# Two-layer attention kernel: bf16 planes stored once and repeated by their loads, and a new order of the work in slots 0 to 6

## Chip, cores and metric

The kernel runs on one core of one Trainium2 chip. The metric is the device time of one launch in microseconds. Below, PE is TensorE, DVE is VectorE, ACT is ScalarE, POOL is GpSimd, and SP is SyncE, which here only issues DMAs.

## The reference

Input x is (8, 128, 64, 64) in fp32. Each of the 8 images goes through two layers.

```
# layer 0 (on the Haar bands of x, 32x32 pixels, N0 = 1024)
ll_out  = sparse attention on ll: 8 heads of 16, q and k l2-normalized,
          keep the top half of each row of q.k, softmax, times v, 1x1 conv, group norm
high    = h + alpha * GN(1x1(silu(GN(depthwise3x3(h)))))      # h: the other three bands
out     = x + 0.1 * inverse_haar(ll + ll_out, high)
out     = out + 0.1 * GN(1x1(gelu(GN(1x1(out)))))
# layer 1 (on 64x64 pixels, N1 = 4096, queries and keys of 16 channels)
attn    = softmax(q.k / 4);  result = gamma * (Wo (v.attn) + bo) + out
```

## The kernel before

**Images overlap.** While image b is in layer 0 (one head per slot), image b-1 is in layer 1 (one chunk of 512 queries per slot). `slots(b, l0, l1)` issues 8 such slots, and `between(f, n, fin, opn)` lies between two images: it finishes layer 0 of image f and opens image n. Image 0 runs alone in layer 0 (`alone`), and the last image alone in layer 1 (`chunks`). The first chunk's maxima are issued by `first`, the last slot by `closing`; the others by `search(h)` and the statements in the loop over h.

**The order is written out by hand.** Each engine has its own list of calls (`search` on PE and DVE, the loop body on ACT), and every engine works strictly in its list's order. They are tied by semaphores.

**A slot, layer 0, head h.** `score` (PE, L446, banks 0 and 1) makes a row block of q.k, `evict` (ACT, L1175) copies it out and sums it, `centre` (DVE) makes thresholds, `count` (ACT, L1183, 24 per head) counts entries above them, and `apart`, `flip`, `eight` (DVE, L1743, L1751, L1760), `match`, `middle`, `threshold` find the exact median. `turn` (PE), `turned` (ACT, L1217) and three DMAs put it as three extra rows under the queries. `half_t` (PE, L514) then makes the transposed scores in halves, `half_e` (ACT, L1235) takes exp, `half_m` (DVE, L1857) masks, and `weigh` (PE, L524) multiplies with v. `score(h + 1, 0)` waits for the last `half_m` of head h - 1.

**A slot, layer 1, chunk j.** `maxima` (PE L548, DVE L1928, 32 per chunk) finds each query's largest score, `parts` and `maxrow` (DVE, PE L555, ACT L1251) split it and move it into QP1, `l1_score` (PE L566), `l1_exp` (ACT L1243) and `l1_weigh` (PE L582) do the attention, and `l1_norm`, `l1_turn` (PE L594), `l1_out` (DVE L1960) end the chunk.

**Planes.** To multiply fp32 values in bf16, q and k are split into three bf16 planes (p0, p1, p2). `TERMS` lists six pairs (plane of q, plane of k), so the contraction has 6 x 16 = 96 rows. Before the change `store_planes` (L286) writes each plane to DRAM once for every term and side that uses it, twelve stores per image, and `load_head` (L279) reads a head's 96 rows with two loads. Layer 1 has one copy of its planes in DRAM (L406) and twelve loads (L410) of 16 rows each into QP1 and KP1. All of these are issued by SP in `between`, after a wait for the last plane (p12) in layer 1. The first `maxima` of a chunk row waits for all of the loads (`qp1`) and for the evicted values (`v1c`); layer 0's first `score` waits for `hq0`.

The one place where the shape of a DMA is set is this (L286, L410):

```python
sp.dma_start(scr0[w, :, j, :, :], PT[:, t, w * N0:w * N0 + N0]).then_inc(s["scrw"], 16)
sp.dma_start(dst[16 * j:16 * j + 16].rearrange("p (j n) -> p j n", j=4),
             scr1[t].rearrange("(j s) n -> s j n", s=32)[16 * w:16 * w + 16]).then_inc(s["qp1"], 16)
```

Of the kernel before, what the change touches and what calls it, by code (L numbers as in the profile page):

```python
# [7 lines left out]
N1 = H * W  # L8
HH = H // 2
N0 = HH * HH  # L10
# [7 lines left out]
TERMS = [(0, 0), (0, 1), (1, 0), (1, 1), (0, 2), (2, 0)]  # L18
# [80 lines left out]
def dwt_attention_kernel(nc, x, qkvT, projT, dw, pwT, w1T, w2T, qk1T, wv, woT, vec, cst, cstT, out,  # L99
# [4 lines left out]
    with ctx:  # L104
# [148 lines left out]
        def kp(h):  # L253
# [4 lines left out]
          scrw1 qp1 v1p v1c m mr mp mt mpt mq st1 e1 pv1 on nt xr0 xr1 y1 out0 out1 dset dimg dpr pimg g1 g2 g3 g4  # L258
# [6 lines left out]
        def _(sp):  # L265
# [10 lines left out]
            def load_head(h):  # L276
                done = s["hq%d" % (h % 3)]
                for w in range(2):
                    sp.dma_start(QK0[0:KS, h % 3, w, :], scr0[w, h].rearrange("j d n -> (j d) n")).then_inc(done, 16)  # L279

            def store_planes(n, t, made):
                sp.wait_ge(s[made], (n + 1) * 2)
                for j, pair in enumerate(TERMS):
                    for w in range(2):
                        if pair[w] == t:
                            sp.dma_start(scr0[w, :, j, :, :], PT[:, t, w * N0:w * N0 + N0]).then_inc(s["scrw"], 16)  # L286
# [2454 lines left out]
```

## Time and profile before

| what | us |
|---|---|
| median of 3 runs | 5668.78 |
| lowest and highest run | 5662.02, 5674.28 |
| span of the profiled execution | 5667.7 |
| span around which the prediction's sum is made, against the median | 1.1 less |

For the profiled execution the page gives its span and no time of its own beside it.

| engine | busy us | share of the span |
|---|---|---|
| PE | 4766.2 | 84% |
| DVE | 4618.9 | 81% |
| ACT | 4256.4 | 75% |
| POOL | 250.6 | 4% |

The 16 DMA engines are busy for 11% of the span. Busy means that an instruction of the engine is executing; PE's ends are modelled. A released wait is named after the instruction whose end released it.

### The profile page before, as it was taken

What the parts mean: (1) busy time and instruction counts of PE and PEld (TensorE: products, weight loads), DVE (VectorE), ACT (ScalarE), POOL (GpSimd) and SP (SyncE); (2) the same over time, 40 slices, a digit from 0 to 9 for tenths busy, and PEclk for the clock granted to TensorE, in tenths of its full rate; (3) what the DMA queues carried; (4) which work ended last, traced back from release to release, by engine and by line L of the source; (5) the groups of instructions that cost most, each with busy time, mean ns of one, the idle gap of its engine ahead of it and who ended that gap; (6) DMA issues with size and microseconds to landing.
All of it is one profiled execution on the core that took longest, in us unless ns stands there. A gap on an engine that the chain in (4) does not pass through costs nothing.

```text
span 5667.7 us, 92692 instructions
## 1 busy us (share of the span) xinstructions
PE 4766.2 (84%) x30180; PEld 3123.3 (55%) x30180; DVE 4618.9 (81%) x9087; ACT 4256.4 (75%) x6779; POOL 250.6 (4%) x125
## 2 busy tenths in 40 slices
PE   4444899988999889988999889998899889997799
PEld 2001366654666456663666546664466636664588
DVE  4887799987999789986999879997799879996553
ACT  3883699948998499966999489884899669994333
POOL 2001000010000200010000100002000100000000
PEclk7555799998999989998999989999899989998899
DMA  1001200012001110012000120011100120001100
GB/s 68 7 11 50 74 15 16 15 56 76 16 20 43 59 43 18 16 61 74 15 15 13 58 76 16 20 43 50 51 16 18 59 75 15 15 13 43 36 12 16
DMA packets 104805, 199.97 MB, mean 35 GB/s; under 512 B 36632, under 2 KB 41656, under 8 KB 100184
## 3 DMA queue, kind: packets, MB, share of 16 engines
q1 hardware_dynamic: 104280, 193.56, 11.1%
q8 instruction: 257, 4.21, 0.3%
q14 instruction: 268, 2.20, 0.1%
HBM read 110.61 MB, written 82.05 MB: 34 GB/s over the span
## 4 chain that ended last, share of the span: by engine, by line
PE 41%; DVE 23%; ACT 15%; issue 14%; SPq 3%; DMA 3%; DVEq 0%; ACTq 0%; POOL 0%; POOLq 0%
PE PS L582 16%; ACT work L1183 7%; PE PS L548 5%; DVE M L1760 4%; DVE MX L1928 4%; PE PS L566 4%; ACT work L1243 3%; DVE work L1751 3%; PE PS L514 3%; PE PS L524 3%; DVE work L1743 2%; PE PS L1057 2%; ACT arena L1175 2%; DVE arena L1857 2%; DMA work<-TPT 1%
## 5 line engine op out<-in xcount | busy, mean ns | idle before, releaser
L582 PEld LDWEIGHTS PS<-V,work 128*128 128x128 f32 x16384 | 2106.7, 193 | 155.8 <-issue 7.0
L582 PE MATMUL PS<-V,work 128*128 128x129 f32 x16384 | 2125.2, 277 | 2.5 <-ACT work L1243 1.2
L1183 ACT ACTIVATE work<-arena,T 128x1024 bf16<-128x1024 f32 x1504 | 1725.8, 1150 | 22.7 <-DVE T L1671 18.8
L1928 DVE TENSOR_REDUCE MX<-PS 128x1 f32<-128x512 f32 x2048 | 1399.3, 687 | 249.6 <-PE PS L548 233.9
L1243 ACT ACTIVATE work<-PS 128x1024 f32<-128x1024 f32 x1024 | 1046.8, 1024 | 334.0 <-PE PS L566 332.3
L548 PE MATMUL PS<-KP,QP 96*128 96x512 bf16 x2048 | 845.5, 414 | 137.3 <-DVE MX L1928 95.3
L566 PE MATMUL PS<-QP,KP 99*128 99x512 bf16 x2048 | 624.6, 387 | 77.5 <-ACT work L1243 54.2
L1175 ACT ACTIVATE arena<-PS 128x1024 f32<-128x1024 f32 x512 | 523.2, 1022 | 216.7 <-PE PS L446 209.5
L1857 DVE SCALAR_TENSOR_TENSOR arena<-PS,work 128x512 f32<-128x512 f32 x896 | 606.2, 684 | 67.3 <-ACT work L1235 65.3
L1760 DVE MAX8 M<-work 128x8 f32<-128x512 f32 x1024 | 648.4, 682 | 1.0
L1235 ACT ACTIVATE work<-PS 128x512 f32<-128x512 f32 x896 | 530.8, 601 | 119.9 <-PE PS L514 116.1
L548 PEld LDWEIGHTS PS<-KP,QP 96*128 96x128 bf16 x2048 | 200.5, 98 | 543.8 <-DVE MX L1928 419.1
L446 PE MATMUL PS<-work 96*128 96x512 bf16 x1024 | 350.5, 428 | 175.2 <-ACT arena L1175 167.2
L514 PE MATMUL PS<-work 99*128 99x512 bf16 x896 | 337.3, 388 | 93.7 <-DVE arena L1857 54.2
L1743 DVE TENSOR_SCALAR work<-arena,T 128x1024 f32<-128x1024 f32 x512 | 378.4, 745 | 2.3
L1751 DVE TENSOR_SCALAR work<-work,FL 128x1024 uint32<-128x1024 uint32 x512 | 375.9, 747 | 1.0
L524 PE MATMUL PS<-arena,VT 128*17 128x256 f32 x4096 | 321.4, 411 | 10.0 <-DVE arena L1849 5.8
L566 PEld LDWEIGHTS PS<-QP,KP 99*128 99x128 bf16 x2048 | 185.0, 99 | 222.6 <-ACT work L1243 126.5
L1183 ACT ACTIVATION_READ_ACCUMULATOR work<-arena,T 128x1 f32 x1504 | 302.9, 201 | 0.0
L446 PEld LDWEIGHTS PS<-work 96*128 96x128 bf16 x1024 | 80.4, 102 | 329.9 <-ACT arena L1175 272.2
L514 PEld LDWEIGHTS PS<-work 99*128 99x128 bf16 x896 | 83.2, 98 | 222.1 <-DVE arena L1857 127.0
L2614 POOL TENSOR_TENSOR work<-work 128x1024 f32<-128x1024 f32 x8 | 22.5, 2814 | 3509.9 <-DMA work<-in_x 3509.9
(193 smaller groups left out, 4160.8 us busy)
## 6 DMA issues: line engine op xcount, KB each, us to landing
scr<-work SPq DMA_DIRECT2D x96, 256.0 KB
work<-scr SPq DMA_DIRECT2D x128, 192.0 KB, 2.8
work<-in_x SPq DMA_DIRECT2D x16, 1024.0 KB, 7.7
arena<-in_x SPq DMA_DIRECT2D x8, 2048.0 KB, 9.9
scrX<-arena SPq DMA_DIRECT2D x8, 2048.0 KB, 14.2
XR<-scrX SPq DMA_DIRECT2D x64, 256.0 KB, 2.8
out<-YO SPq DMA_DIRECT2D x64, 256.0 KB, 2.0
scrL<-work SPq DMA_DIRECT2D x24, 512.0 KB, 2.6
```

Source lines behind the costliest of these rows:

```text
L514: mm(PS[:, c, :], kp(h)[0:KA, 128 * mt:128 * mt + 128], qp(h)[0:KA, 512 * c:512 * c + 512], start=True, stop=True).then_inc(s["st" if c el ...
L548: mm(PS[:, maxbank(c, k, l0), :], QP1[0:KS, c * 512 + 128 * i:c * 512 + 128 * i + 128], KP1[0:KS, 512 * w:512 * w + 512], start=True, stop ...
L566: last = mm(PS[:, pairbanks(k, l0) + t, :], KP1[0:KA, 128 * mt:128 * mt + 128], QP1[0:KA, j * 512:j * 512 + 512], start=True, stop=True)
L582: last = mm(PS[:, 5 + i // 2, 136 * (i % 2):136 * (i % 2) + 129], P1[:, (16 * j + k) % 3, t, 128 * i:128 * i + 128], V1[:, mt, :], start=( ...
L1175: A(scores(h, i), bank2(0), ACT.Copy, scale=0.25, accum_out=SUM[:, h % 2, i:i + 1]).then_inc(s["eva"], 1)
L1183: A(junk[:, m % 2, :], scores(h, i), ACT.Sign, scale=-1.0, bias=T[:, h % 2, i:i + 1], accum_out=CA[:, h % 2, i:i + 1]).then_inc(s["ca"], 1)
L1235: A(JA[:, mt % 2, 512 * c:512 * c + 512], PS[:, c, :], ACT.Exp, scale=0.25).then_inc(s["e" if c else "eh"], 1)
L1243: A(P1[:, (16 * j + k) % 3, :, :].rearrange("p t n -> p (t n)"), PS[:, u:u + 2, :].rearrange("p a n -> p (a n)"), ACT.Exp, scale=0.25).the ...
L1751: cp.did(V.tensor_scalar(JDu[:, c, :], JDu[:, c, :], FL[:, h % 2, i:i + 1].bitcast(u32), None, ALU.bitwise_xor))
L1760: cp.did(V.max(M8[:, i, a, :], JD[:, c, 512 * a:512 * a + 512]))
L1857: V.scalar_tensor_tensor(scores(h, mt)[:, 512 * c:512 * c + 512], PS[:, c, :], 0.0, JA[:, mt % 2, 512 * c:512 * c + 512], ALU.is_ge, ALU.m ...
L1928: V.reduce_max(MX[:, c % 2, i, w:w + 1], PS[:, maxbank(c, k, l0), :], AX.X).then_inc(s["mr"], 1)
```

## The change

The planes of layer 0 are kept once in DRAM (scr0 by plane, partition, side) and stored by one DMA per plane. A head's rows are put together by seven loads, some of which read a plane two or three times, or read two planes at once. `TERMS` is reordered so that rows that share a plane lie together. Layer 1's planes are stored in rows of 8 KB, each plane as soon as it exists, and loaded by seven DMAs in place of twelve. Waits on the counts of these semaphores are adapted. Head 0 of the next image is loaded before its third plane is ready; rows of that plane go from SBUF to SBUF.

The lists of slots 0 to 6 on PE, DVE and ACT have the same calls in another order. `first`, `closing`, `alone`, `chunks` and `between` on these engines are as before.

```diff
-TERMS = [(0, 0), (0, 1), (1, 0), (1, 1), (0, 2), (2, 0)]
+TERMS = [(0, 0), (0, 1), (0, 2), (1, 0), (1, 1), (2, 0)]
-        scr0 = nc.dram_tensor("scr0", [2, NH, len(TERMS), HD, N0], bf16, kind="Internal").ap()
-        scr1 = nc.dram_tensor("scr1", [3, 128, N0], bf16, kind="Internal").ap()
+        scr0 = nc.dram_tensor("scr0", [3, 128, 2, N0], bf16, kind="Internal").ap()
+        scr1 = nc.dram_tensor("scr1", [3, 32, N1], bf16, kind="Internal").ap()
...
-            def load_head(h):
+            def load_head(h, parts=(0, 1, 2)):
                 done = s["hq%d" % (h % 3)]
-                for w in range(2):
-                    sp.dma_start(QK0[0:KS, h % 3, w, :], scr0[w, h].rearrange("j d n -> (j d) n")).then_inc(done, 16)
-
-            def store_planes(n, t, made):
+                d = slice(HD * h, HD * h + HD)
+                q, k = QK0[0:KS, h % 3, 0, :], QK0[0:KS, h % 3, 1, :]
+                if 0 in parts:
+                    sp.dma_start(q[0:48], scr0[0, d, 0, :].unsqueeze(0).to_broadcast([3, HD, N0])).then_inc(done, 16)
+                    sp.dma_start(k[80:96], scr0[0, d, 1, :]).then_inc(done, 16)
+                if 1 in parts:
+                    sp.dma_start(k[0:32], scr0[0:2, d, 1, :]).then_inc(done, 16)
+                    sp.dma_start(k[48:80], scr0[0:2, d, 1, :]).then_inc(done, 16)
+                    sp.dma_start(q[48:80], scr0[1, d, 0, :].unsqueeze(0).to_broadcast([2, HD, N0])).then_inc(done, 16)
+                if 2 in parts:
+                    sp.dma_start(q[80:96], scr0[2, d, 0, :]).then_inc(done, 16)
+                    sp.dma_start(k[32:48], scr0[2, d, 1, :]).then_inc(done, 16)
+
+            def store_plane(n, t, made):
                 sp.wait_ge(s[made], (n + 1) * 2)
-                for j, pair in enumerate(TERMS):
-                    for w in range(2):
-                        if pair[w] == t:
-                            sp.dma_start(scr0[w, :, j, :, :], PT[:, t, w * N0:w * N0 + N0]).then_inc(s["scrw"], 16)
+                sp.dma_start(scr0[t].rearrange("p w n -> p (w n)"), PT[:, t, :]).then_inc(s["scrw"], 16)
+
+            def head0_late():
+                for w, row in ((0, 80), (1, 32)):
+                    sp.dma_start(QK0[row:row + HD, 0, w, :], PT[0:HD, 2, w * N0:w * N0 + N0]).then_inc(s["hq0"], 16)
...
                 if opn:
-                    store_planes(n, 0, "p0")
-                    store_planes(n, 1, "p1")
-                    store_planes(n, 2, "p2")
+                    store_plane(n, 0, "p0")
+                    store_plane(n, 1, "p1")
                     sp.wait_ge(s["vt"], (n + 1) * 2)
                     sp.sem_inc(s["free"], 1)
-                    sp.wait_ge(s["scrw"], (n + 1) * 192)
-                    for h in range(3):
+                    sp.wait_ge(s["scrw"], n * 48 + 32)
+                    load_head(0, (0, 1))
+                    store_plane(n, 2, "p2")
+                    head0_late()
+                    sp.wait_ge(s["scrw"], (n + 1) * 48)
+                    for h in range(1, 3):
                         load_head(h)
                 if fin:
-                    sp.wait_ge(s["p12"], f + 1)
-                    for a in range(3):
-                        sp.dma_start(scr1[a], PT1[:, a, :]).then_inc(s["scrw1"], 16)
-                    sp.wait_ge(s["scrw1"], (f + 1) * 48)
-                    for j, (tq, tk) in enumerate(TERMS):
-                        for w, (t, dst) in enumerate(((tq, QP1), (tk, KP1))):
-                            sp.dma_start(dst[16 * j:16 * j + 16].rearrange("p (j n) -> p j n", j=4),
-                                         scr1[t].rearrange("(j s) n -> s j n", s=32)[16 * w:16 * w + 16]).then_inc(s["qp1"], 16)
+                    for a, made in enumerate(("p10", "p11", "p12")):
+                        sp.wait_ge(s[made], f + 1)
+                        sp.dma_start(scr1[a].rearrange("s (j n) -> j s n", j=4), PT1[:, a, :]).then_inc(s["scrw1" if a < 2 else "scry1"], 16)
+                    sp.wait_ge(s["scrw1"], (f + 1) * 32)
+                    planes = scr1.rearrange("t (w d) n -> t w d n", w=2)
+                    sp.dma_start(KP1[0:32], planes[0:2, 1]).then_inc(s["qp1"], 16)
+                    sp.dma_start(KP1[48:80], planes[0:2, 1]).then_inc(s["qp1"], 16)
+                    sp.dma_start(KP1[80:96], planes[0, 1]).then_inc(s["qp1"], 16)
+                    sp.dma_start(QP1[0:48], planes[0, 0].unsqueeze(0).to_broadcast([3, HD, N1])).then_inc(s["qp1"], 16)
+                    sp.dma_start(QP1[48:80], planes[1, 0].unsqueeze(0).to_broadcast([2, HD, N1])).then_inc(s["qp1"], 16)
+                    sp.wait_ge(s["scry1"], (f + 1) * 16)
+                    sp.dma_start(KP1[32:48], planes[2, 1]).then_inc(s["qp1"], 16)
+                    sp.dma_start(QP1[80:96], planes[2, 0]).then_inc(s["qp1"], 16)
...
@@ PE, the loop over h
+                    l1_weigh(h - 1, 15, (0,))
+                    last_weigh(h, 7)
+                    l1_weigh(h - 1, 15, (1,))
                     maxrow(h)
...
```

**SP in `between`, layer 1's planes.** Here QP and KP are QP1 and KP1, arena holds PT1 and X1, scr is scr1. Before, three stores and the first of twelve loads:

```order
L406 DMA scr<-arena 128x1024 x3
L407 REGISTER_ALU
L410 DMA QP<-scr 16x4x1024
L410 DMA KP<-scr 16x4x1024
...
L413 ISA
```

After:

```order
L420 DMA scr<-arena 4x32x1024 x3
L421 REGISTER_ALU
L423 DMA KP<-scr 32x1x4096
L424 DMA KP<-scr 32x1x4096
L425 DMA KP<-scr 16x4096
L426 DMA QP<-scr 48x1x4096
L427 DMA QP<-scr 32x1x4096
L428 REGISTER_ALU
L429 DMA KP<-scr 16x4096
L430 DMA QP<-scr 16x4096
```

Four loads now fill 32 or 48 rows each, three fill 16 rows, and the store's outermost dimension in DRAM is 4.

**ACT at the end of a slot.** L1235 (L1249 after) is `half_e`, L1183 (L1196) is `count`, L1251 (L1265) is `maxrow`, L1175 (L1188) is `evict` of the next head, L1243 (L1257) is `l1_exp`. Before:

```order
L1235 ACTIVATE work<-PS 128x512
L1182 REGISTER_ALU
L1183 ACTIVATE work,CA<-arena,T 128x1024
L1235 ACTIVATE work<-PS 128x512
L1250 REGISTER_ALU
L1251 ACTIVATE MPT<-PS 12x128
L1203 ISA
L1175 ACTIVATE arena,SUM<-PS 128x1024
L1240 REGISTER_ALU
L1243 ACTIVATE work<-PS 128x1024
```

After:

```order
L1196 ACTIVATE work,CA<-arena,T 128x1024
L1249 ACTIVATE work<-PS 128x512
L1195 REGISTER_ALU
L1196 ACTIVATE work,CA<-arena,T 128x1024
...
L1264 REGISTER_ALU
L1265 ACTIVATE MPT<-PS 12x128
L1217 ISA
L1188 ACTIVATE arena,SUM<-PS 128x1024
L1217 REGISTER_ALU
L1188 ACTIVATE arena,SUM<-PS 128x1024
```

Three counts now stand between the last `half_e` of the slot and `maxrow` (one is shown, two are left out), and two evictions follow each other.

**PE at the end of a slot.** L555 (L574 after) is `maxrow`, L582 (L601) is `l1_weigh`, L524 (L543) is `weigh`, L446 (L465) is `score` of the next head, L594 (L613) is `l1_turn`. Before:

```order
L514 MATMUL PS<-work 128x512
L555 MATMUL PS<-identb,MP 12x128
L573 REGISTER_ALU
L582 MATMUL PS<-V1,work 128x129 x8
L524 MATMUL PS<-arena,VT 17x256 x12
L473 ISA
L446 MATMUL PS<-work 128x512 x2
L594 MATMUL PS<-cons,ON 128x128 x4
```

After:

```order
L601 MATMUL PS<-V1,work 128x129 x8
L574 MATMUL PS<-identb,MP 12x128
L492 ISA
L465 MATMUL PS<-work 128x512 x2
L543 MATMUL PS<-arena,VT 17x256 x12
L613 MATMUL PS<-cons,ON 128x128 x4
L482 REGISTER_ALU
L465 MATMUL PS<-work 128x512 x2
```

The next head's first score stands ahead of three `weigh` calls now, and its second one behind `l1_turn`.

## Rows read from the trace of the kernel before

**Rows 1.** The page's first line.
```profile
span 5667.7 us, 92692 instructions
```
**Rows 2.** Busy time by stretch of one slot: us, PE, PEld, DVE, ACT, POOL busy; PE clock, DMA share, GB/s.
```profile
1498.10:1561.90 63.80, 58.72 (x430) 41.77 (x428) 59.09 (x122) 59.21 (x100) 0.00 (x0) 1.00 0.06 19
...
1498.10:1528.40 30.30, 26.76 (x185) 18.73 (x184) 28.82 (x62) 28.70 (x48) 0.00 (x0) 1.00 0.06 22
1528.40:1534.00 5.60, 4.75 (x35) 3.73 (x33) 3.75 (x8) 5.34 (x10) 0.00 (x0) 1.00 0.01 2
1534.00:1558.80 24.80, 24.10 (x179) 17.43 (x177) 23.92 (x46) 24.15 (x42) 0.00 (x0) 1.00 0.06 15
1558.80:1561.90 3.10, 3.10 (x37) 1.89 (x36) 2.60 (x8) 1.01 (x2) 0.00 (x0) 1.00 0.19 47
```
**Rows 3.** Waits in two slots, 1498.1 to 1625.6: us in total, times, longest.
```profile
ACT arena L1175 <- PE PS L446: 10.2, 7, 2.7
...
DVE MX L1928 <- PE PS L548: 4.0, 8, 0.9
```
**Rows 4.** ACT in that slot: start, us, instruction, idle before it and releaser.
```profile
1529.13 0.25 ACT L1217 ACTIVATE TPT<-PS 24x128 bf16<-24x128 f32 x1
...
1530.42 1.13 ACT L1183 ACTIVATE work<-arena,T 128x1024 bf16<-128x1024 f32 x1
...
1533.04 0.60 ACT L1235 ACTIVATE work<-PS 128x512 f32<-128x512 f32 x1 [0.26 <-PE PS L514]
...
1560.89 1.02 ACT L1175 ACTIVATE arena<-PS 128x1024 f32<-128x1024 f32 x1 [2.70 <-PE PS L446]
```
**Rows 5.** DVE in that slot.
```profile
1528.21 0.17 DVE L1843 TENSOR_TENSOR TP<-TR,TP 128x8 bf16<-128x8 f32 x1
...
1534.00 0.68 DVE L1857 SCALAR_TENSOR_TENSOR arena<-PS,work 128x512 f32<-128x512 f32 x1
...
1557.43 0.74 DVE L1743 TENSOR_SCALAR work<-arena,T 128x1024 f32<-128x1024 f32 x1
1558.11 0.69 DVE L1857 SCALAR_TENSOR_TENSOR arena<-PS,work 128x512 f32<-128x512 f32 x1
```
**Rows 6.** PE at the end of that slot.
```profile
1556.84 2.05 PE L582 MATMUL PS<-V,work 128*128 128x129 f32 x16
1558.82 1.49 PE L524 MATMUL PS<-arena,VT 128*17 128x256 f32 x24
1560.24 0.61 PE L446 MATMUL PS<-work 96*128 96x512 bf16 x2
```
**Rows 7.** SP's DMA issues between images 1 and 2: start, us, issues.
```profile
1290.92 13.92 SPq L286 DMA_DIRECT2D scr<-work  x12
...
1317.86 1.32 SPq L406 DMA_DIRECT2D scr<-arena  x3
```
**Rows 8.** Stretches in which one kind of DMA runs; last two columns: DMA share, GB/s.
```profile
11.00:13.00 2.00, 0.00 (x0) 0.00 (x0) 0.00 (x0) 0.00 (x0) 2.00 (x1) 1.00 1.00 422
...
1305.00:1309.40 4.40, 2.52 (x6) 1.06 (x6) 4.40 (x5) 3.77 (x5) 0.00 (x0) 1.00 0.50 195
...
1208.00:1210.00 2.00, 2.00 (x18) 1.72 (x17) 1.00 (x2) 1.49 (x3) 2.00 (x2) 1.00 0.42 143
```
**Rows 9.** The three planes' last instructions, layer 0 (p1, p2), layer 1 (p12).
```profile
1291.28 2.00 ACT L1518 ACTIVATE work<-work 128x1024 bf16<-128x1024 f32 x2
...
1300.77 1.21 DVE L2409 TENSOR_TENSOR work<-work 128x1024 bf16<-128x1024 f32 x1
...
1316.61 1.23 DVE L2371 TENSOR_TENSOR arena<-arena 128x1024 bf16<-128x1024 f32 x1 [0.26 <-ACT arena L1478]
```
**Rows 10.** PE's first maxima after the loads, images 1/2 and the last.
```profile
1338.21 0.59 PE L548 MATMUL PS<-KP,QP 96*128 96x512 bf16 x2 [0.47 <-ACT V L1484]
1339.37 20.71 PE L548 MATMUL PS<-KP,QP 96*128 96x512 bf16 x30 [0.57 <-DVE MX L1928]
...
5288.58 1.01 PE L548 MATMUL PS<-KP,QP 96*128 96x512 bf16 x2 [13.08 <-DMA KP<-scr]
```

More of the change, by code:

```diff
@@ L435, in _ @@
             for i in range(3):
-                sp.wait_ge(s["hq%d" % i], images * len(range(i, NH, 3)) * 32)
+                sp.wait_ge(s["hq%d" % i], images * len(range(i, NH, 3)) * 112)
             sp.wait_ge(s["dls"], images * 48)
@@ L472, in score @@
                     if i == 0:
[L473 removed]
+                        pe.wait_ge(s["hq%d" % (h % 3)], (b * len(range(h % 3, NH, 3)) + h // 3 + 1) * 112)
                     products(h, i)
@@ L694, in search @@
                     l1_score(h - 1, 10)
                     half_t(h - 1, 1, 1)
+                    maxima(h, 20)
+                    l1_weigh(h - 1, 9, (1,))
+                    half_t(h - 1, 2, 0)
+                    maxima(h, 21)
                     weigh(h - 1, 0)
-                    maxima(h, 21)
-                    l1_weigh(h - 1, 9, (0,))
-                    half_t(h - 1, 2, 0)
+                    weigh(h - 1, 1)
+                    half_t(h - 1, 2, 1)
                     maxima(h, 22)
-                    l1_weigh(h - 1, 9, (1,))
@@ L702, in search @@
-                    half_t(h - 1, 2, 1)
-                    maxima(h, 23)
-                    weigh(h - 1, 1)
                     l1_score(h - 1, 11)
                     half_t(h - 1, 3, 0)
-                    maxima(h, 24)
+                    maxima(h, 23)
                     l1_weigh(h - 1, 10, (0,))
                     half_t(h - 1, 3, 1)
+                    maxima(h, 24)
+                    l1_weigh(h - 1, 10, (1,))
                     maxima(h, 25)
-                    l1_weigh(h - 1, 10, (1,))
@@ L914, in score0 @@
                         pe.wait_ge(s["kon"], n + 1)
-                        pe.wait_ge(s["hq0"], (n * len(range(0, NH, 3)) + 1) * 32)
+                        pe.wait_ge(s["hq0"], (n * len(range(0, NH, 3)) + 1) * 112)
                     products(0, i)
@@ L1377, in slots @@
                     count(h, 1, 5)
+                    l1_exp(h - 1, 9)
                     half_e(h - 1, 0, 0)
+                    half_e(h - 1, 0, 1)
                     count(h, 1, 6)
-                    half_e(h - 1, 0, 1)
-                    count(h, 1, 7)
                     half_e(h - 1, 1, 0)
                     half_e(h - 1, 1, 1)
-                    count(h, 2, 0)
+                    count(h, 1, 7)
                     half_e(h - 1, 2, 0)
@@ L1387, in slots @@
                     half_e(h - 1, 2, 1)
+                    count(h, 2, 0)
+                    l1_exp(h - 1, 11)
+                    half_e(h - 1, 3, 0)
+                    half_e(h - 1, 3, 1)
                     count(h, 2, 1)
-                    half_e(h - 1, 3, 0)
-                    l1_exp(h - 1, 11)
-                    half_e(h - 1, 3, 1)
                     count(h, 2, 2)
+                    count(h, 2, 3)
                     half_e(h - 1, 4, 0)
@@ L1395, in slots @@
                     half_e(h - 1, 4, 1)
-                    count(h, 2, 3)
                     half_e(h - 1, 5, 0)
@@ L2043, in search @@
                     apart(h, 4)
+                    maxima(h + 1, 1)
+                    centre(h + 1, 0)
+                    apart(h, 5)
                     maxima(h + 1, 2)
-                    apart(h, 5)
+                    flip(h, 5)
                     maxima(h + 1, 3)
-                    centre(h + 1, 0)
-                    flip(h, 5)
+                    eight(h, 5)
                     maxima(h + 1, 4)
-                    eight(h, 5)
+                    flip(h, 4)
                     maxima(h + 1, 5)
-                    flip(h, 4)
+                    eight(h, 4)
@@ L2053, in search @@
+                    maxima(h + 1, 6)
                     apart(h, 7)
-                    maxima(h + 1, 6)
-                    eight(h, 4)
                     maxima(h + 1, 7)
                     apart(h, 6)
-                    flip(h, 7)
                     maxima(h + 1, 8)
                     flip(h, 6)
+                    maxima(h + 1, 9)
+                    flip(h, 7)
                     centre(h + 1, 1)
-                    maxima(h + 1, 9)
-                    eight(h, 6)
+                    update(h + 1, 0, 0)
@@ L2064, in search @@
                     maxima(h + 1, 10)
                     eight(h, 7)
-                    update(h + 1, 0, 0)
                     maxima(h + 1, 11)
+                    eight(h, 6)
+                    maxima(h + 1, 12)
                     match(h)
-                    maxima(h + 1, 12)
+                    maxima(h + 1, 13)
                     middle(h)
-                    maxima(h + 1, 13)
                     threshold(h)
                     maxima(h + 1, 14)
+                    update(h + 1, 0, 1)
```

193 lines of the change are left out of this document (87 added, 106 removed).

## Prediction

> **What bounds the kernel now.** I read the page's first line [rows 1], then the timeline, then busy time by stretch. An image takes a passage between two images and eight slots; seven images are worked on in pairs, so 56 slots carry most of the span. In a slot of 63.8 us three engines are busy for almost the same time: PE 58.7, DVE 59.1, ACT 59.2 us [rows 2]. No engine is the bound alone; the slot is longer than any of them by 4.6 to 5.1 us because they wait for each other in turn. The waits say where [rows 3]: ACT waits for the next head's score, up to 2.7 us at a time, and DVE for PE's maxima, 4.0 us in two slots. I cut the slot into three parts. From the last mask of a head to the median (threshold) of the next, 3.1 + 30.3 us, DVE is busiest. From the threshold's end to the first mask, 5.6 us, a chain runs over PE, ACT and DMAs [rows 4, 5]. In the 24.8 us of the masks all three engines are at 23.9 us or more [rows 2]. Then ACT stands idle for 2.70 us [rows 4]: PE first weighs (2.05 and 1.49 us) and only then makes the score for which ACT waits [rows 6].
>
> In the passage between images the first maxima of layer 1 are the gate: behind them DVE reduces 30 blocks in a row, in 20.71 us, and the next slot can't start earlier [rows 10]. They waited for an eviction of values by ACT, not for planes, in the passage shown; in the last image they waited 13.08 us for the load of the planes [rows 10].
>
> **Change, part 1: the slots.** What ACT does stays the same in amount. The masks' part loses three of ACT's counts, 3 x 1.13 = 3.4 us [rows 4], which now fill the idle time behind the last mask; one `apart` of DVE, 0.68 us from start to the next start [rows 5]; and one of PE's weigh halves. DVE then bounds it: 23.9 - 0.7 = 23.2 us of work, and I add 0.2 for one late handoff: 24.8 becomes 23.4, **-1.4 us**. The part up to the threshold gets that `apart`: 33.4 becomes 34.1, **+0.7**. ACT had 28.7 + 1.0 = 29.7 us of work there [rows 2] and gets 3.4 more while one `l1_exp` of 0.9 us leaves it, so 32.2 us: it fits under 34.1, with 1.9 us left for waits. Part of that is spent, since two evictions now follow each other and the second score stands behind `l1_turn`; following the order I find 1.4 us of idle time there. In the chain over the TPT rows ACT has that `l1_exp` ahead of the first `half_e`: 0.25 + 3.4 + 0.9 = 4.5 us against the 3.91 from 1529.13 to 1533.04, less what ACT waited in it (0.26) and what it can start earlier, since it will already stand ready: **+0.1**. Sum -0.6 us a slot. It applies to the six full distances between two slots of each image, 7 x 6 = 42: **-25 us**. The first boundary of an image gains nothing, as `eight(h, 0)` now stands ahead of `parts` there, and `closing` is as before. Bounds of the term: the best is all of DVE's waits for maxima gone, 2.0 us a slot, -84 us; the worst is that ACT's waits grow past the 1.9 us, say by 0.8 us a slot, +34 us.
>
> **Change, part 2: layer 1's planes.** I go through what the most loaded DMA engine must carry. The twelve old stores to scr0 have an outermost dimension of 8 in DRAM, are queued together (12 issues in 13.92 us) [rows 7], and while they drain the 16 engines have a share of 0.50 at 195 GB/s [rows 8]: 8 of 16 engines, 24.4 GB/s each, and the same 8 for all, since otherwise twelve waiting stores would have filled the rest. The load that repeats scrD for seven heads shows 0.42 [rows 8], close to 7 of 16. So the outermost count of the pattern sets how many engines share a DMA. A load that takes two planes (or one plane twice) then has 2 engines, three copies have 3, layer 1's stores have 4. At a share of 1.00 with 8 KB rows the engines move 422 GB/s [rows 8], 26.4 each, so 0.31 us per 8 KB row; at 24.4 GB/s a 2 KB row takes 0.084 us.
>
> The Trainium skill states the same as a rule, against this change (DMA: Bandwidth & Descriptors, "Why a DMA increments its semaphore by 16 and not by 1"): a DMA issued by SP uses the largest number of engines up to 16 that divides the slowest dimension of both sides, and takes the lowest-numbered ones. By that rule the loads pile up on engines 0 and 1; without it, spread over all engines, part 2 would cost nothing. The 0.50 of the trace agrees with it.
>
> The most loaded engine's queue, image 1 to 2: p1 ends at 1293.3 [rows 9], so head 0 is loaded from about 1296 to 1303; p2 ends at 1302.0 [rows 9], its store has landed by about 1305. Then heads 1 and 2 are loaded: per head four loads give it 16 rows each and three give it one, 67 rows x 0.084 = 5.6 us, so it is busy from 1306 to 1317.3. The three stores of layer 1 (p12 ends at 1317.8) [rows 9] give it 32 rows each, 96 x 0.084 = 8.1 us: 1325.4. The seven loads give it 4 x 16 + 3 = 67 rows of 8 KB, 67 x 0.31 = 20.8 us: 1346.2, and landed by 1346.5. PE could have started at 1338.2 [rows 10]: **8.3 us late**. Nothing hides this, since the 30 maxima, the row of maxima and the first score stand in line behind it. ACT's counts don't absorb it: their thresholds come from DVE updates that stand between these maxima. In the last image the same queue, without head loads, ends 8 to 9 us after the old 5288.6. Eight passages: 8 x 8.3 = **+67 us**. Bounds: the loads can't start before the second plane's store has landed, about 1320, which gives 1341, 3 us late (+24); at 21 GB/s per engine the queue ends near 1351, 13 us late (+104). If the engine count is not what I read, the term is 0.
>
> **Small parts.** Layer 0's stores fall from twelve to three, and head 0 is loaded earlier; PE's wait for it in the passage is covered, because ACT evicts layer 1's first planes before it needs that score: 0. A head's seven loads in a slot are issued behind the maxima rows and have 30 us until anything behind them is needed: 0. PE's clock, 1.00 in the slot [rows 2], will fall to its lower level (1.2 GHz) while PE waits for the loads; maxima at 0.69 us each are paced by DVE, so it costs nothing there.
>
> **Sum.** -25 + 67 = +42 us on the profiled execution's 5667.7; it lies 1.1 us under the median of the runs, 5668.8, which gives **5711 us**. About 0.2% (11 us) is what a measurement of this kernel can tell from no change.
>
> **The rivals.**
> - *Planes in time.* The loads run on different engines, or on all 16. For it: a store drawn up with 128 rows on both sides runs on all 16 engines, and nothing in the trace shows a pattern with an outermost count of 2. Against it: the 0.50 and 0.42 [rows 8]. Only the slots' gain is left: 5668.8 - 25 = 5644. It decides from 1338.2 on: if the loads land before that, this is the case. Chance 0.20. This is the other side of my forecast.
> - *The slots give much more.* All DVE waits go, 42 x 2.0 = 84 us, against 67: 5652. The three engines are balanced at 59 us, which speaks for room down to 61.4 us; against it speaks that DVE's maxima pass through one PSUM bank, a round trip each. Break-even is 67/42 = 1.6 us a slot. Chance 0.10.
> - *The slots give nothing or lose.* The second eviction waits for `l1_turn`, which waits for `l1_norm`, and DVE now has one `eight` ahead of it. ACT's idle time of 2.70 us moves there. At no gain 5668.8 + 67 = 5736; at 0.8 us a slot lost, 5769. It decides once ACT waits more than 1.9 us up to the threshold. Chance 0.17.
> - *Forecast*, both parts as worked out: 0.53.
>
> **The numbers.** The forecast's own range is 5668 to 5736, from the bounds of 3 to 13 us with the slots near -0.6. The range 5636 to 5745 adds most of the first two rivals and the milder half of the third; it leaves out some 0.15. Faster by over 0.2%: nearly all of "planes in time" and half of "much more", 0.22. Within 0.2%: 0.10, from the low end of the forecast and the rest of these. Slower: 0.68.
>
> **What the next profile would show.** Right: the first maxima of each passage wait for a DMA into KP1 or QP1, 8 us, at a DMA share near 2/16 over some 20 us; the last image's wait is over 20 us instead of 13.08. A slot takes 63.2 us; ACT has no idle time ahead of the first eviction and about 1.4 us ahead of the second. Wrong: maxima released by ACT's eviction of V as before, or a slot at 63.8 us or above, or at 62 us and below.

## The result and the profile after the change

The changed kernel takes 5750.4 us (median of 4 runs, 5739.3 to 5753.1) against 5665.4 us of the kernel before (4 runs, 5652.9 to 5674.3): a ratio of 1.0151, 95% interval 1.0131 to 1.0172, so **1.5% slower**. Forecast were 5711 us and a range up to 5745: the sign was right, the loss was twice as large.

The page's first line and its groups for the maxima, for the eviction and for one DMA, with the maxima's group of the kernel before behind them, then the time of each slot part (columns as in [rows 2]). The last number of a group is the engine's idle time ahead of it, in us:

```profile
span 5737.5 us, 92907 instructions
...
L567 PE MATMUL PS<-KP,QP 96*128 96x512 bf16 x2048 | 845.7, 414 | 258.0 <-DVE MX L1942 117.6
...
L1188 ACT ACTIVATE arena<-PS 128x1024 f32<-128x1024 f32 x512 | 524.3, 1024 | 116.7 <-PE PS L465 106.7
...
scrX<-arena SPq DMA_DIRECT2D x8, 2048.0 KB, 26.0
```
```profile
L548 PE MATMUL PS<-KP,QP 96*128 96x512 bf16 x2048 | 845.5, 414 | 137.3 <-DVE MX L1928 95.3
```
```profile
1510.90:1540.70 29.80, 28.24 (x195) 19.75 (x193) 28.12 (x61) 28.32 (x45) 0.00 (x0) 1.00 0.08 23
1540.70:1546.30 5.60, 4.20 (x27) 3.04 (x28) 3.98 (x10) 5.12 (x10) 0.00 (x0) 1.00 0.02 3
1546.30:1570.00 23.70, 23.04 (x169) 16.14 (x169) 22.74 (x46) 22.44 (x38) 0.00 (x0) 1.00 0.06 15
1570.00:1574.10 4.10, 4.10 (x43) 2.35 (x42) 3.89 (x12) 3.15 (x7) 0.00 (x0) 1.00 0.02 4
```

This is the slot of [rows 2]: 63.2 us now against 63.8. The masks' part went from 24.8 to 23.7, the two parts up to the threshold from 33.4 to 33.9 together, the chain stayed at 5.6. ACT at the slot's end (start, us, instruction, idle before it):

```profile
1568.01 0.60 ACT L1249 ACTIVATE work<-PS 128x512 f32<-128x512 f32 x1 [0.45 <-PE PS L533]
1568.50 1.14 ACT L1196 ACTIVATE work<-arena,T 128x1024 bf16<-128x1024 f32 x1
...
1571.90 0.25 ACT L1265 ACTIVATE MPT<-PS 12x128 bf16<-12x128 f32 x1
1572.06 1.00 ACT L1188 ACTIVATE arena<-PS 128x1024 f32<-128x1024 f32 x1
...
1574.32 1.02 ACT L1188 ACTIVATE arena<-PS 128x1024 f32<-128x1024 f32 x1 [1.17 <-PE PS L465]
```

Three counts (L1196) follow the last `half_e`; the first eviction has no idle time ahead of it (2.70 us in [rows 4]), the second 1.17 us. ACT's wait for the score in the slot fell from 6.4 to 1.2 us.

Between the images the planes are late. SP's issues, PE's first maxima of images 1/2 and of the last, and stretches of the DMAs (last two columns: share, GB/s):

```profile
1315.37 4.01 SPq L420 DMA_DIRECT2D scr<-arena  x3
1325.86 0.67 SPq L423 DMA_DIRECT2D KP<-scr  x1
...
1329.56 0.42 SPq L430 DMA_DIRECT2D QP<-scr  x1
1330.27 0.38 SPq L432 DMA_DIRECT2D scrX<-arena  x1
```
```profile
1351.37 1.03 PE L567 MATMUL PS<-KP,QP 96*128 96x512 bf16 x2 [11.19 <-DMA QP<-scr]
...
5357.13 1.01 PE L567 MATMUL PS<-KP,QP 96*128 96x512 bf16 x2 [27.47 <-DMA QP<-scr]
```
```profile
1317.00:1326.00 9.00, 5.36 (x18) 3.15 (x19) 1.56 (x3) 5.86 (x11) 0.00 (x0) 0.58 0.26 87
1331.00:1336.00 5.00, 1.82 (x16) 1.47 (x16) 0.17 (x2) 5.00 (x10) 0.00 (x0) 0.95 0.94 347
1338.00:1342.00 4.00, 2.18 (x10) 1.87 (x9) 0.65 (x4) 3.90 (x9) 0.00 (x0) 0.50 0.18 78
1342.20:1343.20 1.00, 0.00 (x0) 0.00 (x0) 0.00 (x0) 1.00 (x2) 0.00 (x0) 0.50 0.14 57
```

PE now waits 11.19 us for the load, in the last image 27.47 instead of 13.08 [rows 10]. While the stores run, the share is 0.26, four engines of 16; 1331 to 1336 is mostly the store of X1, which runs on all of them; then three engines are left (0.18), then two (0.14), at 57 GB/s.

Where the time went, by the starts of `l1_out`'s last DVE step and of PE's first maxima. A distance runs from one slot's `l1_out` to the next one's; the last distance of an image is its closing distance, and a passage runs from the last `l1_out` to PE's first maxima of the next image. Sums over the profiled executions, in us; "first maxima" runs from the start of the program:

```
                               before   after   slots alone (e1)   planes alone (e2)
first maxima, image 1           672.0   683.1       670.9              685.2
42 distances between slots     2691.4  2645.3      2645.0             2698.4
7 closing distances             412.2   418.4       427.7              406.1
7 passages to the first maxima  839.2   930.9       850.0              927.2
8 from maxima to first out      786.4   793.7       795.1              787.4
```

After against before: slots -46 (1.10 us each, not 0.6), but closings +6 and the way from the maxima to the first output +7; the eight passages +103 (11.1 for the first, 91.7 for seven), 12.9 us each, not 8.3. Together this is +70, as the spans of the two profiled executions have it; the medians lie 85 us apart, since the profiled execution of the changed kernel is the fastest of its four.

### The profile page after: what moved, and what is told of

Same layout as the page of the kernel before. It is cut to its first block, busy times and chain, and to the rows that moved or that the text cites. A ratio compares the mean times of both kernels' runs of the same rounds, so it can differ in the third digit from the quotient of the medians.

```text
span 5737.5 us, 92907 instructions
## 1 busy us (share of the span) xinstructions
PE 4809.5 (84%) x30180; PEld 3105.8 (54%) x30180; DVE 4594.7 (80%) x9087; ACT 4261.6 (74%) x6779; POOL 250.7 (4%) x125
## 4 chain that ended last, share of the span: by engine, by line
PE 37%; DVE 31%; issue 13%; ACT 9%; DMA 6%; SPq 2%; DVEq 1%; POOL 0%; ACTq 0%; POOLq 0%
PE PS L601 15%; DVE MX L1942 8%; DVE M L1774 5%; PE PS L567 5%; PE PS L585 3%; DMA QP<-scr 3%; DVE work L1757 3%; DVE work L1765 3%; ACT work L1196 3%; PE PS L533 2%; PE PS L543 2%; DVE arena L1871 2%; ACT work L1257 2%; PE PS L1070 2%; PE PS L980 1%
## 5 line engine op out<-in xcount | busy, mean ns | idle before, releaser
L601 PEld LDWEIGHTS PS<-V,work 128*128 128x128 f32 x16384 | 2110.4, 193 | 155.8 <-ACT work L1257 24.0
L601 PE MATMUL PS<-V,work 128*128 128x129 f32 x16384 | 2135.3, 277 | 2.5 <-ACT work L1257 1.2
L1196 ACT ACTIVATE work<-arena,T 128x1024 bf16<-128x1024 f32 x1504 | 1711.9, 1142 | 98.6 <-DVE T L1715 87.0
L1257 ACT ACTIVATE work<-PS 128x1024 f32<-128x1024 f32 x1024 | 1040.7, 1018 | 336.1 <-PE PS L585 324.9
L1871 DVE SCALAR_TENSOR_TENSOR arena<-PS,work 128x512 f32<-128x512 f32 x896 | 600.4, 685 | 72.6 <-ACT work L1249 65.4
L1249 ACT ACTIVATE work<-PS 128x512 f32<-128x512 f32 x896 | 510.4, 593 | 172.2 <-PE PS L533 165.7
L1188 ACT ACTIVATE arena<-PS 128x1024 f32<-128x1024 f32 x512 | 524.3, 1024 | 116.7 <-PE PS L465 106.7
L465 PE MATMUL PS<-work 96*128 96x512 bf16 x1024 | 352.2, 430 | 127.4 <-ACT arena L1188 125.7
L543 PE MATMUL PS<-arena,VT 128*17 128x256 f32 x4096 | 312.6, 411 | 5.8 <-DVE arena L1863 5.8
L1196 ACT ACTIVATION_READ_ACCUMULATOR work<-arena,T 128x1 f32 x1504 | 291.2, 194 | 0.0
L465 PEld LDWEIGHTS PS<-work 96*128 96x128 bf16 x1024 | 76.9, 102 | 270.2 <-ACT arena L1188 227.2
L543 PEld LDWEIGHTS PS<-arena,VT 128*17 128x17 f32 x4096 | 88.9, 99 | 184.3 <-issue 136.5
```

What stands on the lines that cost most here:

```text
L601: last = mm(PS[:, 5 + i // 2, 136 * (i % 2):136 * (i % 2) + 129], P1[:, (16 * j + k) % 3, t, 128 * i:128 * i + 128], V1[:, mt, :], start=( ...
L1188: A(scores(h, i), bank2(0), ACT.Copy, scale=0.25, accum_out=SUM[:, h % 2, i:i + 1]).then_inc(s["eva"], 1)
L1196: A(junk[:, m % 2, :], scores(h, i), ACT.Sign, scale=-1.0, bias=T[:, h % 2, i:i + 1], accum_out=CA[:, h % 2, i:i + 1]).then_inc(s["ca"], 1)
L1257: A(P1[:, (16 * j + k) % 3, :, :].rearrange("p t n -> p (t n)"), PS[:, u:u + 2, :].rearrange("p a n -> p (a n)"), ACT.Exp, scale=0.25).the ...
L1871: V.scalar_tensor_tensor(scores(h, mt)[:, 512 * c:512 * c + 512], PS[:, c, :], 0.0, JA[:, mt % 2, 512 * c:512 * c + 512], ALU.is_ge, ALU.m ...
```

## The experiments

**e1 and e2: each part alone.** e1 takes only the lists of PE, DVE and ACT from the change, e2 only the stores, loads and TERMS.

> The new order of the slots alone, with the old planes, stores and loads. Theory A (what was predicted, -0.6 us at each of 42 full distances between slots): 5640 us, distances of 63.2 us. Theory B (read off the trace after the change: distances between the last DVE steps of two slots 1.0 us shorter, but the last distance of an image 1.4 us longer and the first 0.7 us longer, and both of these due to the order, not to the planes): -40 + 9 + 6, also about 5640 us, but with that split in the trace. Theory C (as B, but the longer first and last distances come from the planes' loads): 5625 us, with the closing distance at 58.1 us as before. In all of them the first maxima of layer 1 come at the old distance of about 124 us after the last slot.

> The new planes, stores and loads alone, with the old order of the slots. If the two parts add up: the first maxima of layer 1 come 11 to 14 us later in each of eight passages, about +100 us, so 5765 us, with the distances between slots at 63.8 us as before. Rival (the new order of the slots made the passages longer too, the loads only 8.3 us each as predicted): +67 us, 5732 us. If the closing distance is 59.5 us here, it is the loads that lengthen it.

Measured: e1 5647.6 us, ratio 0.9973 (0.9962 to 0.9983); e2 5778.1 us, 1.0204 (1.0187 to 1.0221). The parts are -17 and +113 us; together +96 where the whole is +85, a difference within the three intervals. The table shows the longer closings in e1, not in e2: they come from the order, so theory B of e1 holds in kind. Its time was 8 us over the one given; in its trace closings grew by 2.2 us and passages by 1.5 us each. In e2 the eight passages cost 101 us, 12.7 each: the rival (8.3) falls.

**e3: layer 1's loads on 16 engines.**
```diff
-sp.dma_start(KP1[0:32], planes[0:2, 1]).then_inc(s["qp1"], 16)
...
+for t in (0, 1, 2):
...
+for j, (tq, tk) in enumerate(TERMS):
+    if tk == t:
+        sp.dma_start(KP1[16 * j:16 * j + 16], planes[t, 1]).then_inc(s["qp1"], 16)
+    if tq == t:
+        sp.dma_start(QP1[16 * j:16 * j + 16], planes[t, 0]).then_inc(s["qp1"], 16)
```


> The changed kernel, with layer 1's seven loads written as twelve of 16 rows of 8 KB each; what is stored and where stays the same, and so do the four-engine stores. Theory (the outermost count of the pattern sets how many DMA engines work): all loads run on 16 engines, 1.57 MB in about 4 us behind the last store at 1326, landed by 1333, so PE's first maxima wait for ACT's eviction again and the passages lose their 11 to 14 us: 5645 us. Rival (the rows of 8 KB, the repeated reading of one DRAM region or the later issue is the cost, whatever the engines): the passages stay within 3 us of the changed kernel, 5725 to 5750 us.

Measured: 5654.9 us, ratio 0.9984 (0.9974 to 0.9994). The same bytes from the same place, 96 us faster than the changed kernel: the count of engines is what the planes cost. But the loads landed later than expected, and PE still waits for them:

```profile
1330.89 1.03 PE L567 MATMUL PS<-KP,QP 96*128 96x512 bf16 x2 [1.95 <-DMA QP<-scr]
```
```profile
1318.00:1329.00 11.00, 7.32 (x44) 5.79 (x42) 0.78 (x6) 9.77 (x19) 0.54 (x1) 0.79 1.02 134
1331.00:1336.00 5.00, 4.21 (x8) 0.69 (x7) 4.30 (x8) 5.00 (x7) 0.00 (x0) 0.50 0.96 398
```
The twelve loads took over 11 us, not 4: all 16 engines are busy, at only 134 GB/s, and right behind them, at the same share, the store of X1 moves 398 GB/s. So the share of busy engines does not say what they move.

**e5: the store of X1 moved.** It shares the lowest engines with the loads; here it is issued behind the stores to scrL.
```diff
-                    sp.wait_ge(s["x2"], (f + 1) * 4)
-                    sp.dma_start(scrX[bass.ds(f, 1)].rearrange("a c n -> c (a n)"), X1).then_inc(s["xs"], 16)
                 if opn:
                     for o in range(3):
...
+                if fin:
+                    sp.wait_ge(s["x2"], (f + 1) * 4)
+                    sp.dma_start(scrX[bass.ds(f, 1)].rearrange("a c n -> c (a n)"), X1).then_inc(s["xs"], 16)
```


> The changed kernel, with the store of X1 to scrX (128 rows of 16 KB) issued behind the three stores to scrL instead of right behind layer 1's loads. Theory A (the loads share the two lowest engines with this store, which costs them its 8 rows per engine, 131 KB at 26 GB/s = 5 us in each of 8 passages): first maxima 5 us earlier in every passage, 5710 us. Rival (a DMA engine finishes the earlier loads first, so that the later store costs them nothing and the lateness is their own rate): unchanged, 5750 us.

Measured: 5750.1 us; from the last slot to the first maxima 135.7 us, 135.5 in the changed kernel. Nothing; theory A falls. The store is issued over 20 us behind the first load, 4.4 us in the changed kernel, and in both PE starts 25.7 us behind that load (mean of six passages). The trace of the changed kernel says the same: from 1342 us to the end of the loads the 8 KB packets of the last two engines follow each other every 0.31 us, with none of the store's between them. A version in which the store waits until the loads have landed (e4) has no measurement.

**e6, e15: fewer rows on the lowest engines.** e6 writes `KP1[0:32]` as two loads of 16 rows, e15 also `KP1[48:80]`.

> The changed kernel, with only the load of the first two key planes (KP1 rows 0 to 31) written as two loads of 16 rows. It takes 15 of 67 rows of 8 KB off the two lowest engines. Theory (the most loaded engine's queue, 0.31 us per row): 4.7 us less per passage, first maxima about 130.8 us after the last slot instead of 135.5, 5713 us. Theory with the scrX store interleaved row by row: the same or up to 6 us. Rival (the loads' lateness is set by something all share, such as the landing of the stores or the issue): under 1 us per passage, 5745 us.

> The changed kernel, with both loads of the first two key planes (KP1 rows 0 to 31 and 48 to 79) written as two loads of 16 rows each: 37 rows of 8 KB are left on the lowest engine instead of 67. Theory (0.33 us per row): 10 us less per passage than the changed kernel's 135.5, 125.5 us from the last slot to the first maxima, about 5675 us. Rival (the three-engine and single loads, or the issue, set it by then): 129 us or more, over 5700 us.

Measured: e6 5715.4 us, the passage 130.4 us instead of 135.5 (mean of six): -5.1 us, near the 4.7 of the queue of the most loaded engine. e15 5705.2 us, 130.2 us: by the passage the second dose gave 0.2 us, and the rival's number holds. But a passage also holds work that has nothing to do with the loads. Measured from the first load's issue to PE's first maxima, image 1 to 2, first e6, then e15:

```profile
1322.55 0.77 SPq L424 DMA_DIRECT2D KP<-scr  x2
1344.24 1.03 PE L568 MATMUL PS<-KP,QP 96*128 96x512 bf16 x2 [6.70 <-DMA QP<-scr]
```
```profile
1326.47 0.78 SPq L424 DMA_DIRECT2D KP<-scr  x2
1346.30 1.03 PE L569 MATMUL PS<-KP,QP 96*128 96x512 bf16 x2 [5.82 <-DMA QP<-scr]
```
The mean of six passages is 25.7 us in the changed kernel, 21.6 in e6 and 20.1 in e15: the doses gave 4.1 and 1.5 us. The medians say the same, 35 and 10 us less over eight passages. Why they are not the 4.7 each of the queue shows here:

```profile
1329.00:1333.00 4.00, 1.92 (x15) 1.41 (x14) 0.00 (x0) 4.00 (x8) 0.00 (x0) 0.99 1.00 133
```
A load of 16 rows holds all 16 engines for 1 us where a row of 8 KB takes 0.31 alone. Two of them in place of a load of 32 rows take 16 rows from the lowest engines (5 us) and give back two of about 1 us, so the sum is 3 us gained per dose. In e6 the time from the first 8 KB packet to the end of the last fell by that, from 23.2 to 20.1 us; the other 1 us is that the first packet starts 0.9 us behind the issue instead of 1.9. In e15 the packets' time fell by another 1.4 us only. Why the second dose gives half of the sum stays open.

**e7, e8: what stands ahead of the loads.** e7 issues the loads of heads 1 and 2 behind layer 1's planes; e8 writes each store of layer 1 as four stores of 32 rows, `scr1[a, :, N0 * j:N0 * j + N0]` from `PT1[32 * j:32 * j + 32, a, :]`.

> The changed kernel, with the loads of heads 1 and 2 issued behind layer 1's planes and the scrX store instead of ahead of them. Plane 0 of layer 1 is made at 1315.2 and plane 1 at 1317.6, and its stores were issued within 0.2 us of that, so SP gains nothing; what goes is the head loads' packets on the lowest engines ahead of the stores. Theory (queue of the engine): stores of planes 0 and 1 land 3 us earlier, loads issued at 1323 instead of 1325.9, first maxima 3 us earlier, 5726 us. Rival (the engine had drained the head loads by then, 128 rows of 2 KB on four engines take their own 7 us): unchanged, 5750 us.

> The changed kernel, with each of layer 1's three stores written as four stores of 32 rows each (16 engines instead of 4), into the same layout; the seven loads stay as they are. Theory: the lowest engines carry 3 x 8 rows of 2 KB instead of 3 x 32, 6 us less, but twelve issues take SP 0.5 us each; loads issued at 1322 to 1323, first maxima 3 to 5 us earlier, 5720 us. Rival (stores aren't on the path): unchanged, 5750 us.

Measured: e7 5745.6 us (ratio 1.0134, 1.0107 to 1.0162), the passage 135.3 us: the head loads ahead of the stores cost next to nothing (the planes' loads are issued 10.0 us behind the first store instead of 10.5), the rival holds. From there to the maxima it takes 26.8 us instead of 25.7 (mean of six passages); why was not followed. e8 5710.7 us (1.0068, 1.0049 to 1.0088), 131.2 us: 4.3 us less. The loads are issued at 1320.15, 6.9 us behind the first store, where the changed kernel took 10.5:

```profile
1313.21 5.59 SPq L421 DMA_DIRECT2D scr<-arena  x12
1320.15 0.61 SPq L424 DMA_DIRECT2D KP<-scr  x1
```

**e9, e13, e14: why the closing is longer.** Ahead of the closing no maxima of a next head stand between the row of maxima and layer 1's second score. PE waits for the DMA that brings this row (e1):

```profile
2470.38 0.63 PE L524 MATMUL PS<-arena,VT 128*17 128x256 f32 x8
2472.29 0.60 PE L566 MATMUL PS<-QP,KP 99*128 99x512 bf16 x2 [1.28 <-DMA QP<-MPT]
```
e9 turns the row on PE ahead of `l1_weigh` and `last_weigh` in that one slot (`if h == NH - 1: maxrow(h)`); e13 also moves ACT's three counts behind its copy of the row; e14 is e13 with e3's loads.
```diff
                 def closing():
                     maxrow(NH - 1)
+                    count(NH - 1, 2, 5)
+                    count(NH - 1, 2, 6)
+                    count(NH - 1, 2, 7)
...
-                    count(h, 2, 5)
-                    count(h, 2, 6)
-                    count(h, 2, 7)
+                    if h < NH - 1:
+                        count(h, 2, 5)
+                        count(h, 2, 6)
+                        count(h, 2, 7)
```


> The new slots with the old planes (as in the run of the slots alone, 5647.6 us), but in the slot ahead of the closing the row of maxima is turned on PE where it was before, ahead of last_weigh. Theory (the closing's second score waits 1.28 us for the DMA into QP of rows that hang on this turning): closing distances back from 59.5 to about 58.1 us where the clock is 0.97, 7 x 1.3 = 9 us less, 5638 us. Rival (the closing is longer because TensorE's granted clock is lower there, 0.92 to 0.95): unchanged, 5648 us.

> The changed kernel with twelve loads of 16 rows (5654.9 us) and the row of maxima where it was in the slot ahead of the closing. As above: 9 us less, 5646 us; rival: unchanged, 5655 us.

> The kernel with the new slots, the old planes and the row of maxima early in the slot ahead of the closing (5644.4 us), now also with ScalarE's last three counts of that slot behind its copy of the row. Theory (the closing's second score waits for the DMA of that row, and the copy stood behind counts of 1.13 us each): no wait for QP<-MPT in the closing, 58.1 us at a clock of 0.97 instead of 59.3, 7 x 1.2 = 8 us less, 5636 us. Rival (another wait takes its place, since DVE's first masks are as late): 59.3 us, 5644 us.

> The same on the changed kernel with twelve loads of 16 rows (5652.3 us with the row early): 8 us less, 5644 us; rival: 5652 us.

Measured: e9 5644.4 us (0.9962, 0.9947 to 0.9977) and e10, the same with e3's loads, 5652.3 us (0.9985, 0.9976 to 0.9994): closings at a clock of 0.97 went from 59.5 us in e1 to between 59.1 and 59.4, about a fifth of what was expected. PE's place for the row was not it; ACT, with its counts, came to it no earlier. e13 5638.2 us (0.9951, 0.9939 to 0.9963) and e14 5648.4 us (0.9971, 0.9961 to 0.9981): closings of 58.3 us at 0.97, and in e13 the score does not wait:

```profile
1146.31 0.63 PE L524 MATMUL PS<-arena,VT 128*17 128x256 f32 x8
1146.86 0.60 PE L566 MATMUL PS<-QP,KP 99*128 99x512 bf16 x2
1148.51 0.63 PE L524 MATMUL PS<-arena,VT 128*17 128x256 f32 x8 [1.04 <-DVE arena L1856]
```
The cause of the 1.2 us is shown, with PE's row early as in e9: the three counts, which fill idle time in every other slot, here stand ahead of a row on which the closing hangs. (The counts' move without e9's was not run.) Most of the gain is given back: the sixth distance, just before the closing, grew from 64.4 us in e1 to 65.2, and from 64.6 in e3 to 65.4 in e14. From e9 to e13 and from e10 to e14 the total time falls by 6 and 4 us, but the intervals overlap; it is the traces that show the step.

**e11, e12: what in the order gives the gain.** e11 puts PE's `score(h + 1, 0)` behind the three weighs again; e12 keeps PE and DVE new and gives ACT its old list.

> The new slots with the old planes (5647.6 us), but PE makes the next head's first score behind the three last weighs (3.5 us) again, as in the kernel before. Theory A (the gain is that ACT's counts now fill the time in which it waits for this score; its place on PE is free): distances within 0.2 us of 62.7, 5640 to 5655 us. Theory B (the gain comes from the earlier score): ACT waits again ahead of the first eviction, 1 to 2 us per slot, 5690 to 5730 us.

> The new order on PE and DVE with ScalarE's list of before, with the old planes. Theory (ScalarE's counts in the masks' part and its idle time behind it are what the slot gained by; the three lists have to fit each other): the gain is lost and the lists no longer match, distances of 63.8 to 65 us, 5665 to 5720 us. Rival (PE's and DVE's order alone made the gain): distances of 62.7, 5648 us.

Measured: e11 5643.7 us (0.9965, 0.9952 to 0.9977), the first five distances 62.8 us on average, 62.7 in e1, and ACT's idle time ahead of the evictions is the same (4.9 us, 4.7 in e1, from 1500 to 1950 us): the place of the score is free, since ACT's counts cover it. e12 6249.4 us (1.1031, 1.1008 to 1.1055), far beyond what theory gave. The same busy times now stand in a slot of 75.1 us, in which the engines wait in turn:

```profile
1689.60:1764.70 75.10, 59.74 (x429) 41.69 (x428) 58.93 (x123) 59.59 (x98) 0.00 (x0) 1.00 0.05 14
```
```profile
PEld PS L566 <- ACT work L1237: 7.8, 6, 2.5
...
ACT work L1237 <- PE PS L566: 6.3, 3, 3.8
DVE MX L1922 <- PE PS L548: 6.2, 7, 1.7
```
So the three lists are one object; how much each move of ACT's list gives by itself these two runs don't tell.

**e16, e17: the rest of the lateness, and the slow loads.** e16 is e14 with e8's stores. e17 lays scr1 out as [2, 3, 16, N1], so that `KP1[0:32]` and `KP1[48:80]` are each one load of 32 rows on 16 engines, with 24 stores of 16 rows.

> The version with twelve loads of 16 rows and the counts behind the row (5648.4 us), now with each of layer 1's stores as four of 32 rows. Theory (the four-engine stores, which land 8 to 9 us after their issue, are what keeps the first maxima of the last image 3.3 us and of single passages up to 2 us later than with the old planes): stores land 3 to 4 us earlier, no wait for QP1 or KP1 in the passages between images, the last image's passage at 104 us instead of 107.3, together 5 to 10 us less, 5640 us. Rival (twelve issues on SP eat it up): 5648 us.

> A measurement of one rate: the same with a layout of scr1 in which the first two key planes lie together, so that KP1 rows 0 to 31 and 48 to 79 are each one load of 32 rows of 8 KB on 16 engines; the stores are 24 of 16 rows, which makes the passages later and the kernel slower than 5648 us (about 5690 us). Theory A (a load is limited by how many partitions it writes): the loads of 32 rows move over 200 GB/s at a DMA share of 1.00, their packets of 8 KB take 0.5 to 0.6 us each, while those of the loads of 16 rows stay at 0.95 us and 134 GB/s. Theory B (the limit is in reading one DRAM region by 16 engines at once, or in packets of 8 KB): 0.95 us and 134 GB/s for both.

Measured: e16 **5634.5 us**, ratio 0.9951 (0.9939 to 0.9962). The loads are issued 7.4 us behind the first store, PE's first maxima between images wait for no DMA (1329.04 below, as in the other five), and the last image's passage is 103.4 us, 107.3 in e14.

```profile
1327.67 1.44 PE L961 MATMUL PS<-GGH,indT 32*128 32x2 f32 x6
1329.04 1.03 PE L568 MATMUL PS<-KP,QP 96*128 96x512 bf16 x2
```
This version beats the kernel before by 0.5%, and stores the planes once. The old planes with the new order (e13) have the same ratio, so nothing is gained from the new planes themselves.

e17, a single execution, 5636.9 us, not the 5690 expected (the 24 stores, issued 0.46 us apart, landed in time). First the two loads of 32 rows, then loads of 16:

```profile
1316.00:1317.90 1.90, 1.42 (x10) 0.93 (x10) 0.00 (x0) 1.90 (x5) 0.00 (x0) 1.00 0.97 250
1318.50:1323.50 5.00, 2.50 (x12) 2.07 (x13) 0.00 (x0) 4.58 (x10) 0.00 (x0) 0.78 1.02 154
```
At a full share 250 against 154 GB/s, and most packets of the same 8 KB take 0.58 against 0.845 us: theory A, by the partitions that are written, holds in direction; B falls. The Trainium skill (SBUF — State Buffer, "Door 1: The DMA port swizzle (why `[64,N]` ≈ `[32,N]`)") says that a DMA's rate depends on how many of 16 ports of 27.2 GB/s its partitions reach, in groups of four neighbouring partitions. An estimate from that page: 109 GB/s for 16 rows, 218 for 32. The traces agree in the step from one to the other, not in the size: 131 to 154 and 250 GB/s. The stretches hold several loads one behind the other, into different partitions, so the rate of a single load isn't isolated here.

## Why the prediction was right in sign and wrong in size

- **Engine count from the outermost dimension: right.** Shares of 0.26, 0.18 and 0.14, and e3's 96 us. "Planes in time" (0.20) is refuted for these loads.
- **Stores: the number is right by luck.** Their end was worked out as 1325.4, behind the head loads on the same engines; the first load was issued at 1325.86. But the head loads cost next to nothing (e7), only the first two stores had landed by then, and the third one's last packet ended at 1328.07. SP's issue of the second store at 1317.6 and the 8.2 us until both had landed set the loads' issue, and e8 gained 4.3 us there.
- **"67 x 0.31 = 20.8 us: 1346.2, and landed by 1346.5": the term that failed.** The mechanism is right, its size is not. From issue to PE's start it is 25.5 us: 1325.86 to 1351.37. The first packet of 8 KB starts at 1327.9, 2.0 us behind the issue, where the sum has none. It isn't a fixed cost: with the stores on 16 engines (e8) it is 1.4 us, and where the first load is one of 16 rows (e3, e6, e15, e16) 0.9 us. So some 0.6 of the 2.0 go with the four-engine store that still runs on the same engines (until 1328.07), and 0.5 with the load's shape; neither was tested alone. The packets then take 23.0 us, not 20.8. A packet alone takes 0.309 us, as taken, and from about 1333 on they do so; the difference lies ahead of it, where the loads of 16 rows run on all 16 engines beside the others and single packets take up to 1.3 us (in e3, with such loads alone, 0.98). Another 0.5 goes until PE starts. Together 4.7 us, about the difference between 8.3 and the 12.9 measured; times 8, 37 us. With these the forecast would have been 5748, above the range's top of 5745. The last image's passage grew by 13.6 us, not by 8 to 9.
- **The range.** The bound of 13 us (+104) did hold the term, but the sum was made wrongly: 5668.8 + 104 - 25 is 5748, where the forecast's own range says 5736. So the 5745 leaves out what the stated bounds allow.
- **Slots, "-0.6 a slot": right for its slot, too small for the rest.** The slot of [rows 2] went from 63.8 to 63.2, part by part as worked out (masks -1.1 against -1.4, up to the threshold +0.5 against +0.7, chain 0.0 against +0.1). It was the one that gained least; its neighbours went from 63.7 to 62.6, 62.9 and 62.3. Mean 1.10 us.
- **"The first boundary gains nothing, and closing is as before": wrong.** An unchanged list behind a changed slot starts from another state. Closings +1.4 us at an equal clock, 1.2 of it by the three counts (e13), and 1.1 us per image from the maxima to the first output (e1), whose cause was not followed. They ate the slots' surplus: with passages 1.5 us longer (at a lower clock, see the end) they leave e1's -17 us against the -25 predicted.
- **ACT's idle time: right**, 0 and 1.17 us against 0 and 1.4. The first maxima's wait was given as 8 us, over 20 in the last image: 11.19 and 27.47.
- **Against the rivals.** The distances gained 46 us, between the forecast's 25 and the 84 of "the slots give much more", and nearer to the forecast. "The slots give nothing or lose" (5736 to 5769) held the time by luck: the slots gained, the loads cost more.

## What to carry to other kernels

When one DMA replaces several, look at the outermost count of both sides first: it sets how many engines carry it, and the most loaded engine's rows times the time of one are its cost; add the time from issue to first packet, here 0.9 us ahead of a load on 16 engines and 1.4 to 2.4 ahead of one on two, wherever the loads wait for a landing. A list that fills idle time fills it only where nothing behind it is awaited, so the boundaries on both sides of a repeated stage are to be costed even if their own lists don't change. Take a stage's gain from several of its repeats, not from one, and the gain of a DMA from its issue to the instruction that waits for it, since the length of the whole stage also moves for other reasons.

## What the runs showed of the hardware

- A DMA share of 1.00 stood beside 134 GB/s (loads of 8 KB rows into 16 partitions), 154 and 250 GB/s (into 16 and 32, e17) and 398 GB/s (128 partitions). The old loads with rows of 2 KB into 16 partitions show 132 GB/s at a full share too, so it is not the rows' size.
- The length of a passage goes, roughly, with TensorE's granted clock, which is 1.00 in the slots and swings between its levels of 1.2 and 2.4 GHz here. The shortest passage between images of before, its longest, and the longest of e1, of about the same work, are:

```profile
4531.40:4649.30 117.90, 100.52 (x372) 52.80 (x370) 79.91 (x152) 68.49 (x100) 9.20 (x7) 0.93 0.28 75
1876.20:2000.60 124.40, 103.42 (x372) 55.62 (x371) 80.30 (x152) 68.68 (x100) 9.20 (x7) 0.90 0.29 75
```
```profile
2530.20:2658.70 128.50, 107.36 (x372) 56.26 (x366) 80.29 (x152) 68.56 (x100) 9.20 (x7) 0.87 0.27 70
```
  PE is busy for 100.5 to 107.4 us with the same 372 instructions, so the lower mean isn't only that it waits more. Closings follow the mean clock less well: e1 has 59.5 us at 0.97 and 60.0 to 63.8 at 0.92 to 0.95, but before has 58.1 us at 0.97 and at 0.94, and 61.1 at 0.94 too. What moves the clock from one passage to the next was not tested. Single passages of one kernel differ by 5 us and more, so a difference of 0.1% between two of these kernels means little.
